# Seven half-size products for eight in the second stage's matrix product

## The reference

```python
def xattn(query, key):
    a = einsum('bqd,bkd->bqk', query, key)
    return einsum('bqk,bkd->bqd', softmax(a, axis=-1), key)

def ffn(x, weight_real, bias):
    alpha = mean(abs(weight_real), axis=1, keepdims=True)
    return einsum('bsi,oi->bso', x, alpha * sign(weight_real)) + bias

x = x + tanh(g_xattn) * xattn(layernorm(x), ctx)
x = x + tanh(g_ffn) * ffn(layernorm(x), weight, bias)
```

## Time and profile before

| | |
|---|---|
| time, median of 3 runs | 1171.07 us (1170.62 to 1171.31) |
| the profiled execution: its time, its span | 1170.11 us, 1168.3 us |
| mean granted clock of TensorE | 0.963 |
| busy: PE, DVE, ACT, POOL | 1041.8, 761.7, 347.5, 230.7 us |

### The profile page before, as it was taken

How to read it: one execution, slowest core, us unless ns; L and a number is a source line. 1 busy time by engine, 2 the same in 40 slices (tenths; PEclk the granted TensorE clock), 3 DMA queues, 4 the chain that set the end, 5 groups by cost and what they waited for, 6 DMA issues and landing times.

```text
span 1168.3 us, 14014 instructions
## 1 busy us (share of the span) xinstructions
PE 1041.8 (89%) x5680; PEld 511.3 (44%) x5680; DVE 761.7 (65%) x1072; ACT 347.5 (30%) x278; POOL 230.7 (20%) x301
## 2 busy tenths in 40 slices
PE   0325968899979999999889999999799999999998
PEld 0313534344434444444444444444344444444443
DVE  3536868676676776676586667766586666677531
ACT  1723755222222222222232222222132222222100
POOL 0004110122221112222222211122222221113100
PEclk9966989899989999999989999999999999999999
DMA  8769471785556555556645655555745565553221
GB/s 261 169 111 193 148 180 37 184 213 139 136 140 141 119 127 118 144 145 144 157 114 144 145 139 118 127 122 144 181 114 131 134 145 144 127 126 73 72 77 68
DMA packets 287776, 159.25 MB, mean 136 GB/s; under 512 B 276448, under 2 KB 276448, under 8 KB 276960
## 3 DMA queue, kind: packets, MB, share of 16 engines
q1 hardware_dynamic: 285408, 141.58, 52.1%
q10 hardware_dynamic: 2304, 16.78, 4.6%
HBM read 55.58 MB, written 33.55 MB: 76 GB/s over the span
## 4 chain that ended last, share of the span: by engine, by line
PE 75%; issue 11%; DVE 5%; DMA 3%; POOL 2%; SPq 2%; ACT 1%; ACTq 0%; POOLq 0%; DVEq 0%
PE y_ps L808 66%; PE s_ps L778 4%; PE c_ps L793 4%; DMA xn<-in_ctx_dram 3%; SPq L274 1%; POOL xr L360 1%; DVE x1n L561 1%; DVE kmax L613 1%; SPq L266 0%; DMA xr<-in_x_dram 0%; DVE xr L591 0%; DVE prob L581 0%; DVE qn L556 0%; ACT xn L407 0%; DVE st L549 0%
## 5 line engine op out<-in xcount | busy, mean ns | idle before, releaser
L808 PE MATMUL y_ps<-wsign,x1t 128*128 128x512 fp8e4 x4096 | 924.6, 382 | 16.8 <-DMA x1t<-x1n 13.4
L808 PEld LDWEIGHTS y_ps<-wsign,x1t 128*128 128x128 f16 x4096 | 400.7, 99 | 496.4 <-issue 23.5
L420 ACT ACTIVATE xn<-xr,nm,r 128x2048 f32<-128x2048 f32 x32 | 67.0, 2092 | 352.6 <-POOL nm L353 350.8
L591 DVE SCALAR_TENSOR_TENSOR xr<-c_ps,coef,xr 128x512 f32<-128x512 f32 x128 | 95.7, 747 | 98.2 <-PE c_ps L793 98.2
L603 DVE TENSOR_TENSOR ytmp<-y_ps,alpha_b 128x512 f32<-128x512 f32 x128 | 86.2, 673 | 101.2 <-PE y_ps L808 101.2
L360 POOL TENSOR_TENSOR xr<-xr,bias_b 128x2048 f32<-128x2048 f32 x32 | 144.5, 4516 | 4.4 <-ACT xn L420 4.4
L561 DVE SCALAR_TENSOR_TENSOR x1n<-xn,x1n 128x2048 f16<-128x2048 f32 x32 | 132.7, 4147 | 12.3 <-ACT x1n L426 12.3
L793 PE MATMUL c_ps<-kd,pt 128*128 128x512 f16 x256 | 79.9, 397 | 32.3 <-DVE xr L591 31.4
L345 POOL TENSOR_TENSOR ve<-mv,eps 128x1 f32<-128x1 f32 x32 | 8.0, 250 | 498.3 <-DVE mv L598 498.3
L607 DVE TENSOR_TENSOR xr<-ytmp,xr 128x512 f32<-128x512 f32 x128 | 97.2, 759 | 4.4
L594 DVE BATCH_NORM_STATS2 st<-xr 128x6 f32<-128x512 f32 x128 | 88.9, 694 | 4.4
(11 more groups left out here) (61 smaller groups left out, 348.3 us busy)
## 6 DMA issues: line engine op xcount, KB each, us to landing
xr<-in_x_dram SPq DMA_DIRECT2D x32, 1024.0 KB, 6.9
out_dram<-xr SPq DMA_DIRECT2D x31, 1024.0 KB, 4.8
xr<-n_L_ffn_weight_real_dram ACTq DMA_DIRECT2D x8, 1024.0 KB, 6.2
spare<-n_L_ffn_weight_real_dram ACTq DMA_DIRECT2D x8, 1024.0 KB, 4.9
xn<-in_ctx_dram SPq DMA_DIRECT2D x8, 512.0 KB, 6.6
qt<-qn SPq DMA_TRANSPOSE x64, 4.7
bias_b<-in_L_ffn_bias_dram SPq DMA_DIRECT2D x1, 1024.0 KB, 8.7
x1t<-x1n SPq DMA_TRANSPOSE x64, 5.1
```

Source lines behind the costliest of these rows:

```text
L420: nc.scalar.activation(xn2[:, :], xr[:, u % RX, :], ACT.Identity, bias=nm2[:, :], scale=r2[:, :]).then_inc(xn2_set, 1)
L591: nc.vector.scalar_tensor_tensor(out=xr[:, r, chunk(n)], in0=c_ps[:, n % 2, :], scalar=coef[:, 0:1], in1=xr[:, r, chunk(n)], op0=ALU.mult, ...
L808: last = nc.tensor.matmul(y_ps[:, bank_y(t, n), :], x1t[:, t % RT, part, block(k)], wsign[:, k, chunk(n)], start=(k == 0 and part == 0), s ...
```

## The change

Tiles 0 to 3 are multiplied as before (`plain_block`), now with tile 3 behind the three that share the start. Tiles 4 to 31 are multiplied in 14 pairs. For a pair the left matrix has 2 x 2 blocks: A11 and A12 are the left and right half of the columns of the odd tile's normalised rows, A21 and A22 those of the even tile's. The signs have 2 x 2 blocks b11 to b22 in the same way. With S3 = A11 - A21, S1 = A21 + A22, S2 = A22 - S3, S4 = A12 - S2 and t1 = b12 - b11, t2 = b22 - t1, t3 = b22 - b12, n4 = b21 - t2, the four result blocks come from seven products (the scheme of Strassen in Winograd's form). In the order in which PE does them: A11 b11, A12 b21, S3 t3, S2 t2, S1 t1, A22 n4, S4 b22. Each product is 2 chunks n of 512 columns x 8 blocks k x 2 parts, done in halves of 8 matmuls (`half_product`), and adds up in the banks of `BANKS`; ACT copies a bank away where a partial sum is wanted twice (`copy_first`, `copy_third`, `snapshot`), and `finish_pair` on DVE makes the results.

POOL forms S3, S1, S2, S4 (`make_s3` and so on, each 128 x 1024 float32) and t1 and n4 once; DVE forms t2 and t3 once. t1, t2 and n4 lie in buffers that the weight's start has used, t3 overwrites b12 behind tile 3.

The left blocks and the first stage's normalised rows pass in half widths through three slots of `natural`, with high and low part side by side, and one DMA transpose turns both parts of a half (`turn_block`), 11 a pair where there were 8. The order is that of `NAT`. The left blocks land in four slots of `ring_a`. For the very first rows, keys and x1 halves PE does the transposition (`TURNS`). A block of q is normalised twice, by ACT straight into the high part (`direct_high`) and by DVE with `tensor_scalar` into `xn_q` (`rows_q`). From tile 3 on ACT takes the first stage's row statistics in two passes (`sum_rows1`, `square_rows1`). `y_ps` has six banks, `c_ps` one instead of two. `ctx_f` is a buffer of its own; keys are loaded a pair earlier; the largest value of the first keys is found with a PE transposition instead of POOL's reduction. The weight's loads are issued by SP instead of ACT, and ACT takes 11 of the 16 absolute sums. At the start SP asks for x of tile 0 first, then for the keys, the gates, and the weight blocks between tiles of x.

All orders are written anew, for the start in single steps, for the pairs as three patterns: a regular pair, the pair of `KEYS_PERIOD` in which new keys are scaled, and the one behind it. In a regular pair PE does, among the 28 half products: the four chunks of `attend` of the first new tile in front of, behind 2, 4 and 5 halves; those of the second behind 9, 10, 14 and 15; `scores` of two later tiles behind 18 and 24, and `transpose_probs` behind 23 and at the end.

The diff, cut to its core:

```diff
+    PLAIN = 4
...
+    PAIRS_N = (NT - PLAIN) // 2
+    BLOCKS_A = ["A11", "A12", "S3", "S2", "S1", "A22", "S4"]
...
+    KEYS_PERIOD = {(TPB * b - PLAIN) // 2 - 2: b for b in range(1, NB)}
...
+    REGULAR = [("S1", 0, 0), ("A22", 0, 0), ("q", 0, 0), ("q", 0, 1), ("S4", 0, 0), ("q", 1, 0), ("q", 1, 1),
+               ("A11", 1, 0), ("S3", 1, 0), ("S2", 1, 0), ("A12", 1, 0)]
...
+        y_ps = psum("y_ps", [P, 6, BANK])
+        c_ps = psum("c_ps", [P, BANK])
...
+        b11, b12 = wsign[:, 0:HALF, 0:DH], wsign[:, 0:HALF, DH:DO]
+        b21, b22 = wsign[:, HALF:ND, 0:DH], wsign[:, HALF:ND, DH:DO]
+        t1, t2 = [spare[:, i, :].bitcast(F8).rearrange("p (k n) -> p k n", k=HALF) for i in range(2)]
+        n4 = sg[:, :, :].rearrange("p a n -> p (a n)").bitcast(F8).rearrange("p (k n) -> p k n", k=HALF)
+        t3 = b12
+        RIGHT = [b11, b21, t3, t2, t1, n4, b22]
+        BANKS = [0, 4, 2, 0, 0, 2, 0]
...
+            def turn_block(kind, u, h, dst):
+                i = nat(kind, u, h)
+                sp.wait_ge(low_set, i + 1)
+                sp.dma_start_transpose(dst.rearrange("p a k i -> p (a k) i"),
+                                       natural[:, i % RN].rearrange("p a n -> p (a n)")).then_inc(nat_turned[i % RN], 16)
...
+            def make_s3(p):
+                pool.wait_ge(xn2_set, PLAIN + 2 * p + 2)
+                pool.wait_ge(low_set, nat("A11", p) + 1)
+                nc.gpsimd.tensor_tensor(rows_a("S3"), rows_a("A11"), xn_b[:, half(0)], ALU.subtract).then_inc(s_set, 1)
...
+            def make_t1(n):
...
+                nc.gpsimd.tensor_tensor(t1[:, :, cols], b12[:, :, cols], b11[:, :, cols], ALU.subtract,
+                                        saturate=False).then_inc(t1_set, 1)
...
+                    if more:
+                        scale2(f - 1)
+                        make_s3(p + 1)
+                        make_s1(p + 1)
+                        make_s2(p + 1)
+                        make_s4(p + 1)
+                        add_bias(f - 2)
+                        add_bias(f - 1)
...
+            def sum_rows1(u):
...
+                nc.scalar.activation(junk, xr[:, u % RX, :], ACT.Copy, accum_out=sum1[:, :]).then_inc(sum1_set, 1)
+            def square_rows1(u):
...
+                nc.scalar.activation(junk, xr[:, u % RX, :], ACT.Square, bias=mean1[:, :],
+                                     accum_out=sq1[:, :]).then_inc(sq1_set, 1)
...
+            def direct_high(kind, u, h, r, nm):
...
+                nc.scalar.activation(natural[:, i % RN, 0, :], xr[:, u % RX, half(h)], ACT.Identity, bias=nm[:, :],
+                                     scale=r[:, :]).then_inc(high_set, 1)
...
+            def copy_first(p, n):
+                act.wait_ge(y_ready, product_done(p, 0, n))
+                act.wait_ge(y_added, result_read(p - 1, "C12", n) if p > 0 else len(CHUNKS))
+                nc.scalar.copy(snap_a[:, n, :], y_ps[:, n, :]).then_inc(first_set, 1)
...
+                act.wait_ge(y_added, result_read(p, "C11", n))
...
...
...
+                nc.scalar.copy(snap_b[:, n, :], y_ps[:, n, :]).then_inc(snap_set, 1)
...
+            def low(kind, u, h, src):
+                i = nat(kind, u, h)
+                dve.wait_ge(high_set, i + 1)
+                nc.vector.tensor_tensor(natural[:, i % RN, 1, :], src, natural[:, i % RN, 0, :],
+                                        ALU.subtract).then_inc(low_set, 1)
...
+            def rows_q(u, h):
...
+                nc.vector.tensor_scalar(xn_q[:, :], xr[:, u % RX, half(h)], r1[:, 0:1], nm1[:, 0:1], ALU.mult,
+                                        ALU.add).then_inc(xn1_set, 1)
...
+            def finish_pair(p, c, n):
+                j = {"C11": 1, "C22": 4, "C21": 5, "C12": 6}[c]
+                u = PLAIN + 2 * p + (1 if c[1] == "1" else 0)
+                m = n + (2 if c[2] == "2" else 0)
+                r, done = u % RX, result_read(p, c, n)
+                tmp = (snap_b if c == "C21" else snap_a)[:, n, :]
+                x_bank, v_bank, y_bank = y_ps[:, n, :], y_ps[:, 2 + n, :], y_ps[:, 4 + n, :]
+                dve.wait_ge(y_ready, product_done(p, j, n))
+                if c == "C12":
+                    nc.vector.tensor_tensor(tmp, x_bank, alpha_b[:, chunk(m)], ALU.mult).then_inc(y_scaled, 1)
+                    dve.wait_ge(y_scaled, done)
+                else:
+                    if c == "C21":
+                        dve.wait_ge(snap_set, 2 * p + n + 1)
+                        nc.vector.tensor_tensor(tmp, v_bank, snap_b[:, n, :], ALU.add).then_inc(y_scaled, 1)
+                    else:
+                        dve.wait_ge(first_set if c == "C11" else third_set, 2 * p + n + 1)
+                        nc.vector.tensor_tensor(tmp, y_bank if c == "C11" else x_bank, snap_a[:, n, :],
+                                                ALU.add).then_inc(y_scaled, 1)
+                    dve.wait_ge(y_scaled, done)
+                    nc.vector.tensor_tensor(tmp, tmp, alpha_b[:, chunk(m)], ALU.mult).then_inc(y_multiplied, 1)
+                    dve.wait_ge(y_multiplied, 6 * p + 2 * RESULTS.index(c) + n + 1)
+                dve.wait_ge(x1b_set, u + 1)
+                nc.vector.tensor_tensor(xr[:, r, chunk(m)], tmp, xr[:, r, chunk(m)], ALU.add).then_inc(y_added, 1)
...
+                nc.vector.tensor_tensor(t2[:, :, cols], b22[:, :, cols], t1[:, :, cols], ALU.subtract,
+                                        saturate=False).then_inc(t2_set, 1)
...
+                nc.vector.tensor_tensor(t3[:, :, cols], b22[:, :, cols], b12[:, :, cols], ALU.subtract,
+                                        saturate=False).then_inc(t3_set, 1)
...
+                    if more:
+                        attention(f - 2, 0)
+                    finish_pair(p - 1, "C12", 1)
+                    if more:
+                        attention(f - 2, 1)
+                        attention(f - 2, 2)
+                    if p + 1 in KEYS_PERIOD:
+                        key_max(KEYS_PERIOD[p + 1])
+                    if more:
+                        attention(f - 2, 3)
...
+                    finish_pair(p, "C11", 0)
+                    if more:
+                        attention(f - 1, 0)
+                    low_a(p, "A22")
+                    if later:
+                        low_q(f, 0)
+                        low_q(f, 1)
+                    if more:
+                        attention(f - 1, 1)
+                    finish_pair(p, "C11", 1)
+                    if more:
+                        attention(f - 1, 2)
+                        attention(f - 1, 3)
+                    low_a(p, "S4")
+                    if later:
+                        low_q(f + 1, 0)
+                    finish_pair(p, "C22", 0)
+                    if later:
+                        max_logits(f)
+                        low_q(f + 1, 1)
+                        split_probs(f)
+                    if more:
+                        low_a(p + 1, "A11")
+                    finish_pair(p, "C22", 1)
+                    finish_pair(p, "C21", 0)
+                    finish_pair(p, "C21", 1)
+                    if more:
+                        low_a(p + 1, "S3")
+                    if later:
+                        max_logits(f + 1)
+                        split_probs(f + 1)
+                    finish_pair(p, "C12", 0)
+                    if more:
+                        low_a(p + 1, "S2")
+                        low_a(p + 1, "A12")
...
+            def half_product(p, j, n, g):
...
+                        pe.wait_ge(y_scaled, result_read(p - 1, "C12", n) if p > 0 else 13 + n)
+                    if kind == "A12" and p == 0:
+                        pe.wait_ge(out_dve if n else out_act, TURN_PAIRS)
+                        pe.wait_ge(alpha_set, NC)
+                    if kind == "S3":
+                        pe.wait_ge(y_scaled, result_read(p - 1, "C21", n) if p > 0 else 15 + n)
+                    if kind == "S2":
+                        pe.wait_ge(first_set, 2 * p + n + 1)
+                    if kind == "S1":
+                        pe.wait_ge(snap_set, 2 * p + n + 1)
+                    if kind == "A22":
+                        pe.wait_ge(third_set, 2 * p + n + 1)
+                    if kind == "S4":
+                        pe.wait_ge(y_scaled, result_read(p, "C22", n))
+                first = kind in ("A11", "A12", "S3")
+                for k in range(4 * g, 4 * g + 4):
+                    for part in range(2):
+                        last = nc.tensor.matmul(y_ps[:, BANKS[j] + n, :], ring_a[:, slot_a(p, j), part, k, :],
+                                                RIGHT[j][:, k, chunk(n)], start=(first and k == 0 and part == 0),
+                                                stop=(k == HALF - 1 and part == 1), skip_group_check=True)
```

More of the change, by code:

```diff
@@ new lines, in nat, with by_pe, turned_count, turn @@
+    def nat(kind, u, h=0):
+        return NAT.index((kind, u, h))
+    def by_pe(i):
+        kind, u, h = NAT[i]
```

(86 more changed lines are left out.)

1881 lines of the change are left out of this document (1484 added, 397 removed), and 9 rows, old and new, of tables (NAT, TURNS).

## The result

The changed kernel takes 1073.13 us (median of 4 runs, 1071.58 to 1074.29), the kernel before 1170.84 (4 runs, 1169.87 to 1171.31): a ratio of 0.9166, 95% interval 0.915 to 0.9181. The forecast was 1030, the range 990 to 1095, the likeliest case alone 1008 to 1058: the faster side was right, the size 43 us too good.

A forecast was written before the change was run, and what follows sets the result against it. PE was taken as the bound of regular tiles, with losses at new keys and the start: 1170.1 - 96.7 (products) - 28 (keys) - 28 (start) + 14 (blocking) = 1031.4, said as 1030; range 990 to 1095.

The forecast's parts named there:

- +14 for slips: All 14 pairs: VectorE, held back by GpSimd's four sums, delays PE, charged at 1 us a pair.
- A: Pairs: VectorE, blocked by GpSimd's long instructions, becomes the bound at 60 us; about 1082; chance 0.27 with two other rivals.
- B: Pairs: DMA transposes bind, PE waits 3.5 us a pair; 1080; chance 0.27 with two other rivals.
- E: Right-hand combinations and crowded start cancel the start's gain, pairs 0 and 1 slip 20 us; 1079; 0.27 with two others.
- Two signs of being wrong: In the pairs: 59 us or more with PE waiting for C12's read or a transpose; a clock below 1.00.
- Part 1: Pairs on PE: 224 weight matmuls instead of 256, 6.9 us a pair, -96.7 us, if every other engine fits in 55.4.
- Part 2: Tiles with new keys: own buffer, earlier load and scaling under cover of products remove all three stalls, -28 us.
- Part 3: The start: PE turns, reordered loads and ACT row sums bring tile 3 to about 211 from 237.6; -28 us, bounds 0 to -60.
- Parts 4 and 5: Pairs: VectorE needs 45.4 of 55.4 us; GpSimd's 22.8 us can block part of that, bias adds fall beside attention.
- Part 6: Other engines in a pair: ACT 30 and DMA 47 of 55.4 us, no charge; new right-hand combinations priced within the start's range.
- C: Start runs as planned, -60 us, and no pair slips; total 985; chance 0.13.
- D: Pairs: VectorE does nothing during any GpSimd instruction, a pair costs 68.2 us; total 1197, slower; chance 0.06.

The follow-up runs named there:

- the fastest kernel: All-reduce off GpSimd, bias add moved, scores earlier, start's long GpSimd instructions in pieces, next tile's 1/deviation first, on the changed kernel: 1028.76 us, ratio 0.8796.

## Why the prediction was right, and where it was off

**The sum.** 1170.1 - 96.7 (products) - 28 (keys) - 43 (start, to tile 3) - 3 (one tile's attention more done by then) + 75 (slips) = 1074; the profiled execution took 1071.6, and 2 us stay unexplained. The start is 18 better than forecast, the slips 61 worse. **The term that was mis-sized is the +14 for slips**: it priced all fourteen pairs as regular ones at 1 us each, and eight are not. The time lies in the range, which A, B and E had made wide, but by slips that the sum did not price, with part of them paid back by the start: in part luck. Two signs of being wrong came in part: those eight pairs took 59 us or more, and the granted clock was 0.93, 0.97 and 0.95 in pairs 0, 1 and 3. PE's waits there were not the ones named, though: for VectorE's read of C12 it waited 6.3 us in the whole run.

**Part 1** held: 3648 weight products (512 and 3136), 6.9 us a regular pair, shown by the eighth product put back. Its condition, "only while every other engine fits", decided: in pairs 0, 1, 3 and 7 it does not, and by the eighth product (one run) 66.7 of the 96.7 arrive.

**Part 2 is the step behind the slips of pairs 3 and 7.** No transfer of keys is in the way any more, as said. But it asked only for the scaling and two transposes to fit and did not price the maximum over the partitions, 15 to 16 us in GpSimd's order. Before, a tile's mean and variance both came from VectorE; now the mean goes through GpSimd between ScalarE's two statistics passes, and these stand ahead of the copy that frees a PE bank. The three removed give 17.4 back, two unused ones added take 17.7: shown from both sides. The remaining 22 of 39.5 sit in pairs 4, 5, 8 and 9. In pair 4 PE waits 3.78 us for softmax behind a bias add (moving it, with the scores earlier, took 2.8 of that away, but not from the total), 2.09 for the bank copy, and 1.25 and 0.84 for the one bank of attention; a second bank was not tried.

**Part 3**: -28 was too careful; -46 came, with the attention. Its own figures (12 + 126 / 0.75) give 180 for the last weight copy, not 175; it came at 155.8. ScalarE was busy for 92% of the first stretch, where three quarters were chosen. The bounds 0 to -60 held. GpSimd's long instructions hold the start by a further 14: pair 0 begins 14.6 earlier without bias adds (one run), 13.4 with all of them in pieces.

**Parts 4 and 5**: 45.4 and 3 to 6 of blocking against 50.9 measured. The charge of 1 us is right for regular pairs (0.7 to 1.1 over). The run without bias adds shows why: the long instructions lie beside attention there. Part 5's list of what can be blocked was short, though: it named the 512 to 1024 column instructions and took softmax's as free. Those two of 64 columns can be blocked (7.36 and 4.45 us), and stand on PE's path.

**Part 6**: ScalarE 28.0 (30 said), DMA share 0.77 (0.85), transposes 4.5 to landing. "Nothing on PE waits for them before pair 0's third product" looked only at who reads the combinations: inside the third product PE waits 11.18 us for softmax, and softmax waits for `make_n4`.

**The rivals.** A by its mechanism is near (a product less gains nothing), by its size (60 a regular pair) not. B is refuted for PE: over the whole run 0.6 us of waits of its weight loads end with a transpose; ScalarE waited 23.5 us for transposes to free their slots. C's start came halfway. D is refuted by 56.14. E's slip of pairs 0 and 1 happened and was larger (30, it had 20 for the two), but the start did not pay for it.

**Open**: the fastest kernel still slips 45 us, 16 of it in pairs 0 and 1 and 22 in pairs 3 to 5 and 7 to 9. Some is clock: in the changed kernel's pair 0, 13.4 us of waits stand beside a granted clock of 0.93 and 17.7 us lost. How much comes back with the last wait was not measured.

## What to carry to other kernels

Work taken from the bounding engine pays only in the stretches where the others fit: price each kind of stretch, not only the regular one. On a queue that another engine's small results pass through, price an instruction by the distance from its predecessor's end to its successor's start, not by its busy time. Where GpSimd's long instructions meet short VectorE ones on the path, cut them into pieces there, and leave them whole where they lie beside work that isn't blocked. When a run gains a few microseconds, look whether they came in the stretch that was changed.

## What the runs showed of the hardware that was not expected

GpSimd's all-reduce over the partitions of one column is busy for 0.38 to 1.01 us in the profile. In the changed kernel and with the two unused ones, GpSimd's rows show nothing for 6.0 to 8.5 us ahead of it and for 7.2 to 7.6 behind it, though its data is long there; in the kernel before, where GpSimd was idle anyway, it started 0.1 to 0.2 us behind its data. What it does in these gaps the profile doesn't show. One `tensor_scalar` of VectorE on 128x64 took 7.36 us behind a GpSimd instruction of 7.46. GpSimd took 7.46 us for two fp8 inputs of 4096 elements a lane, less than the 9.0 estimated, and in eight pieces 8.48. And a wait costs more than itself, but not always: in pair 3, 7.2 us of waits and 1.4 of slower products behind the long one make most of the 9.0 lost, and the same first wait of 1.9 us in pair 1 was followed by a lower clock in one profile and not in another.
